# Table addresses of a group computed together at the front of a TensorE step, with the next group's register load behind them

## The chip, the cores and the metric

One NeuronCore of one Trainium2 chip runs the whole kernel. Its engines (TensorE or PE, VectorE or DVE, ScalarE or ACT, GpSimd or POOL, SyncE or SP) have an instruction stream each and meet only at semaphores. On TensorE two things must be kept apart: the sequencer, which executes register instructions, waits and branches, and the array, which takes weight loads (PEld) and matmuls (PE) from a queue that the sequencer fills. The metric is device time in microseconds (us) of one execution.

## The reference

A graph of 3125 nodes with 64 features and 100000 edges, sorted by destination. First three message-passing steps, then three relational layers, with a residual and a layer norm after each part:

```python
h = node_state                                   # three steps
for _ in range(MSG_STEPS):
    msg_in = jnp.concatenate([h[src], h[dst], edge_attr], axis=1)
    msg = _mlp(msg_in, W1e, b1e, W2e, b2e)       # silu(x @ W1 + b1) @ W2 + b2
    agg = jax.ops.segment_sum(msg, dst, num_segments=n) / deg
    h = h + _mlp(jnp.concatenate([h, agg], axis=1), W1n, b1n, W2n, b2n)

def _rgcn_layer(x, W, root, b, src, dst, edge_type, n_nodes):   # three layers
    seg = edge_type * n_nodes + dst
    agg = jax.ops.segment_sum(x[src], seg, num_segments=R * n_nodes)
    agg = (agg / jnp.maximum(cnt, 1.0)[:, None]).reshape(R, n_nodes, -1)
    return x @ root + b + jnp.einsum('rni,rio->no', agg, W)
```

`h[src]` and `h[dst]` are gathers, `segment_sum` is a scatter; these are what the loops below do for every edge.

## The kernel before

The edges are sorted on the chip into tiles of 128 (one block of destinations, one span of 256 sources each), and 8 tiles make a group; there are 160 groups, padding included. Node features stand in SBUF as `table`, split into three bf16 parts (192 columns a block). A gather is a matmul with a one-hot matrix as weights: L934 takes the first 128 sources of the tile's span, L935 the next 128 (`table_next` is `table_flat` shifted by one block row), and L938, in the message layers only, the destination block. The column at which a tile reads the table depends on the data, so it stands in a register of TensorE's sequencer.

The six layers share one pattern: `stage(g, u, i)` is one step and does group g. Layers 0 to 2 are the message layers, 3 to 5 the relation layers. The first four groups of a layer are written out, the other 156 run in a loop of 39 turns with four steps each (u = 0 to 3), and two or three steps without gathers end it.

- In a message layer a step has 24 gather matmuls (8 tiles, L934, L935, L938), 8 transposes of the destination one-hots (L948) and 8 matmuls that sum the messages of group g-3 (L968). Then `load_places` (L916) computes the place of the next group's record and loads nine registers with one TENSOR_LOAD: eight table offsets, and the destination's.
- In a relation layer a step has 8 times two gathers (L934, L935) and four sums of group g-2 (L977). `load_places` (L918, eight registers) stands behind tile 3.

At the front of a step, L988 and L990 clamp the loaded registers (`pe.snap`). A tile's table address is then worked out where the matmul is written: a few additions and multiplications of registers that the builder packs into one instruction (FUSED_REGOPS in the profile, ISA in the program's order) ahead of the matmul. L922 to L926 and L931 compute semaphore values for `gather_ready` (the one-hots of this group have been made or loaded) and for the reading of the previous group's gathers. L1016 is the loop's end.

The other engines work on neighbouring groups meanwhile: VectorE adds the gathered parts (L1337, L1341) and, in the first layer, builds the one-hots (L1315, L1316); ScalarE applies the SiLU and casts; GpSimd forms the low parts and accumulates.

Of the kernel before, what the change touches and what calls it, by code (L numbers as in the profile page):

```python
# [22 lines left out]
K3 = 3 * HID  # L23
# [3 lines left out]
def gnn_kernel(nc, x, src, dst, edge_attr, edge_type, W1e, b1e, W2e, b2e, W1n, b1n, W2n, b2n,  # L27
# [22 lines left out]
    LAYERS = 3  # L50
# [19 lines left out]
    with ExitStack() as ctx:  # L70
# [46 lines left out]
        table_flat = table[:].rearrange("p b m k f -> p (b m k f)")  # L117
        table_next = table_flat[:, ROWW:]
# [258 lines left out]
        def done(n):  # L377

            return n + 1 + PRE
# [407 lines left out]
        def _(pe):  # L787
# [100 lines left out]
            for l in range(2 * LAYERS):  # L888
# [24 lines left out]
                def load_places(g, u, l=l):  # L913

                    if l < LAYERS:
                        pe.load(tile_regs[u % 2] + [dst_reg[u % 2]], places[0:1, bass.ds(ROW * g, GT + 1)])  # L916
                    else:
                        pe.load(tile_regs[u % 2], places[0:1, bass.ds(ROW * g, GT)])  # L918

                def gather_ready(g, u, i, l=l):  # L920
                    if l == 0:
                        pe.wait_ge(ohT_made, done(g))  # L922
                    elif isinstance(g, int):
                        pe.wait_ge(hots_loaded[u], 16 * (QUADS * (l - 1) + g // 4 + 1))
                    else:
                        pe.wait_ge(hots_loaded[u], 16 * (QUADS * (l - 1) + 1) + 16 * i)  # L926

                def gather_tile(g, u, j, off, dst_off, l=l):
                    n = l * NG + g
                    if j % 4 == 0:  # L930
                        pe.wait_ge(gat_read, done(2 * (n - 1) + j // 4))  # L931
                    at = gat[:, 256 * j:256 * j + K3]
                    tile = slice(j * P, (j + 1) * P)
                    pe.matmul(at, ohT[u][:, 0, tile], table_flat[:, bass.ds(off[j], K3)], start=True, stop=False)  # L934
                    ins = pe.matmul(at, ohT[u][:, 1, tile], table_next[:, bass.ds(off[j], K3)],  # L935
                                    start=False, stop=l >= LAYERS)
                    if l < LAYERS:
                        ins = pe.matmul(at, ohT[u][:, 2, tile], table_flat[:, bass.ds(dst_off, K3)],  # L938
                                        start=False, stop=True)
                    if j % 4 == 3:  # L940
                        ins.then_inc(gathered, 1)

                def turn_dst_hots(g, u, l=l):

                    n = l * NG + g
                    pe.wait_ge(hot_out, done(n - 2))
                    for j in range(GT):
                        ins = pe.transpose(oh_ps[u % 2][:, j * P:(j + 1) * P], ohT[u][:, 2, j * P:(j + 1) * P],  # L948
                                           ident_b[:])
                    ins.then_inc(turned, 1)  # L950

                def sums_ready(g, u, l=l):
                    n = l * NG + g
                    pe.wait_ge(acc_read, done(n - 2))
                    if l < LAYERS:
                        pe.wait_ge(hot_out, done(n))
                        pe.wait_ge(low_made, done(n))
                        if l == 0:
                            pe.wait_ge(types_made, done(n))
                    else:  # L960
                        pe.wait_ge(oh_made, done(n - LAYERS * NG))
                        pe.wait_ge(gat_read, done(2 * n + 1))

                def sum_messages(g, u, l=l):
                    w = W3 if l == 0 else K3
                    sums_ready(g, u)
                    for j in range(GT):
                        ins = pe.matmul(accp[u % 2][:, 0:w], oh[u][:, j, :], parts[u][:, j, 0:w],  # L968
                                        start=j == 0, stop=j == GT - 1)
                    ins.then_inc(summed, 1)  # L970

                def sums_half(g, u, j):

                    s = u % 2
                    r = j // 2
                    for t in range(4 * (j % 2), 4 * (j % 2) + 4):
                        ins = pe.matmul(accp[s][:, 256 * r:256 * r + K3], oh4[u][:, t, r * P:(r + 1) * P],  # L977
                                        gb[u][:, t, :], start=t == 0, stop=t == GT - 1)
                    if j == GT - 1:
                        ins.then_inc(summed, 1)  # L980

                def stage(g, u, i, l=l):

                    known = isinstance(g, int)
                    gathers = not known or g < NG
                    off, dst_off = [], None
                    if gathers:
                        off = [pe.snap(r, min_val=0, max_val=SPAN * ROWW * (NS - 1)) for r in tile_regs[u % 2]]  # L988
                        if l < LAYERS:
                            dst_off = pe.snap(dst_reg[u % 2], min_val=0, max_val=ROWW * (NB - 1) + K3)  # L990
                        gather_ready(g, u, i)
                    if l < LAYERS:
                        if gathers:
                            for j in range(GT):
                                gather_tile(g, u, j, off, dst_off)
                            turn_dst_hots(g, u)
                        if not known or g >= LAG:
                            sum_messages(g - LAG, (u + 4 - LAG) % 4)
                        if gathers:
                            load_places(g + 1, u + 1)  # L1000
                    else:
                        adds = not known or g >= 2
                        for j in range(GT):
                            if gathers:
                                gather_tile(g, u, j, off, dst_off)
                            if adds:
                                if j == 0:
                                    sums_ready(g - 2, (u + 2) % 4)
                                sums_half(g - 2, (u + 2) % 4, j)
                            if j == 3 and gathers:  # L1010
                                load_places(g + 1, u + 1)

                load_places(0, 0)
                for g in range(4):
                    stage(g, g, 0)
                with pe.Fori(1, QUADS) as i:  # L1016
                    for u in range(4):
                        stage(4 * i + u, u, i)
                for g in range(NG, NG + (LAG if l < LAYERS else 2)):
                    stage(g, g % 4, QUADS)  # L1020
# [427 lines left out]
```

## Time and profile before

| | |
|---|---|
| median of 3 runs | 5863.55 us (5863.24 to 5865.77) |
| the profiled execution: its time | 5864.59 us |
| its span, first to last instruction | 5862.9 us |
| PE busy | 4725.5 us (81%), 47638 matmuls |
| PEld busy | 4058.5 us (69%) |
| DVE busy | 3972.5 us (68%) |
| ACT busy | 2755.2 us (47%) |
| POOL busy | 3395.9 us (58%) |
| mean granted TensorE clock | 0.863 of 2.4 GHz |
| chain that ended last | PE 56%, POOL 15%, issue 10%, DMA 9%, DVE 7% |

Busy time leaves out register, branch, semaphore and DMA-issuing instructions, so a sequencer full of them looks idle. Such time stands in the chain and in the waits as "issue": the engine waited for nothing that another engine did. Matmul durations overlap, since matmuls are pipelined; their pace is read from the distance of their starts. The sequencer's instructions can be had line by line; there TensorE's have the name PEldq and GpSimd's POOLq.

Until about 1500 us the kernel sorts the edges; then the six layers follow, 640 to 800 us each with what lies between them.

### The profile page before, as it was taken

The numbers are of one execution on the slowest core, as the hardware profiler recorded it, in microseconds if no ns is written. First come the engines' busy times: TensorE is split into PE (matmuls) and PEld (weight loads), VectorE is DVE, ScalarE is ACT, GpSimd is POOL, SyncE is SP. The second block draws the span as 40 slices with busy tenths as digits, with TensorE's granted clock in tenths as the row PEclk, the third lists the DMA queues.
The fourth block names the chain that finished last, engine by engine and source line by source line (L and its number), as shares of the span: only waits on it lengthen the run. The fifth ranks groups of instructions, "written<-read, shape, count | busy, mean of one in ns | idle before, by whom it ended". The sixth has DMA issues, their size and how long they took to land.

```text
span 5862.9 us, 173813 instructions
## 1 busy us (share of the span) xinstructions
PE 4725.5 (81%) x47638; PEld 4058.5 (69%) x47639; DVE 3972.5 (68%) x9658; ACT 2755.2 (47%) x4407; POOL 3395.9 (58%) x4499
## 2 busy tenths in 40 slices
PE   2666666660577777888888888899999999999998
PEld 2444444440466665777767777699998999999997
DVE  6444444440589997777767777688875888578885
ACT  1111111112456665677757777555554555455553
POOL 0777777770367775455535555366653666446663
PEclk9755555555799999999999999899998999899997
DMA  8111111117899997777757777244432444234441
GB/s 327 29 29 29 29 29 29 29 28 244 272 312 333 334 334 245 248 264 266 264 176 265 263 265 265 92 133 133 132 120 83 132 132 133 93 109 133 132 133 58
DMA packets 358467, 975.41 MB, mean 166 GB/s; under 512 B 71168, under 2 KB 83796, under 8 KB 358411
## 3 DMA queue, kind: packets, MB, share of 16 engines
q1 hardware_dynamic: 317352, 946.00, 48.9%
q0 software_dynamic: 38400, 28.13, 2.7%
q10 hardware_dynamic: 2658, 0.51, 0.0%
q8 instruction: 37, 0.61, 0.0%
q14 instruction: 20, 0.16, 0.0%
HBM read 774.54 MB, written 199.06 MB: 166 GB/s over the span
## 4 chain that ended last, share of the span: by engine, by line
PE 56%; POOL 15%; issue 10%; DMA 9%; DVE 7%; another core or an unknown queue 2%; ACT 1%; DVEq 0%; POOLq 0%; SPq 0%; ACTq 0%
PE sums L977 21%; POOL recs L517 14%; PE gat L934 10%; PE gat L935 10%; DMA arena<-rows_d 5%; PE gat L938 4%; PE sums L968 4%; DMA arena<-recs 3%; PE sums L948 2%; DMA recs<-arena 2%; DVE arena L1341 1%; PE gat L1060 1%; DVE arena L1316 1%; DVE arena L1337 1%
## 5 line engine op out<-in xcount | busy, mean ns | idle before, releaser
L934 PE MATMUL gat<-table,arena 128*128 x7680 | 1913.4, 249 | 370.8 <-DVE arena L1341 186.7
L935 PE MATMUL gat<-table,arena 128*128 x7680 | 1916.7, 250 | 0.0
L977 PE MATMUL sums<-arena 128*128 128x192 bf16 x15360 | 1887.2, 246 | 0.0
L1357 DVE TENSOR_SCALAR arena<-iota_s,meta_t 128x512 bf16<-128x512 int16 x3840 | 1523.0, 469 | 363.2 <-PE sums L977 363.2
L977 PEld LDWEIGHTS sums<-arena 128*128 128x128 bf16 x15360 | 1325.3, 98 | 0.1
L517 POOL DMA_INDIRECT recs<-arena x800 | 949.8, 1187 | 377.4 <-issue 374.9
L721 ACT CAST arena<-gat 128x768 bf16<-128x768 f32 x960 | 767.0, 799 | 809.3 <-PE gat L935 809.3
L934 PEld LDWEIGHTS gat<-table,arena 128*128 128x128 bf16 x7680 | 747.7, 97 | 548.3 <-issue 482.1
L938 PE MATMUL gat<-table,arena 128*128 x3840 | 959.9, 250 | 0.0
L540 POOL TENSOR_TENSOR arena<-arena 128x512 bf16<-128x512 f32 x480 | 532.6, 1110 | 726.3 <-ACT arena L707 726.0
L1341 DVE TENSOR_TENSOR arena<-arena,gat 128x256 f32<-128x256 f32 x1920 | 812.0, 423 | 65.8
L935 PEld LDWEIGHTS gat<-table,arena 128*128 128x128 bf16 x7680 | 748.0, 97 | 137.2 <-issue 0.4
L592 POOL TENSOR_TENSOR arena<-arena 128x256 f32<-128x256 f32 x480 | 414.5, 864 | 656.7 <-ACT arena L729 655.9
L693 ACT COPY arena<-sums 128x1024 bf16<-128x1024 bf16 x480 | 486.3, 1013 | 518.2 <-PE sums L948 517.8
L1337 DVE TENSOR_TENSOR arena<-gat,arena 128x256 f32<-128x256 f32 x960 | 402.8, 420 | 263.4 <-PE gat L938 262.1
L832 PE MATMUL gat<-arena 25*125 25x39 bf16 x800 | 232.0, 290 | 401.8 <-DVE arena L1179 401.8
L656 ACT COPY arena<-gat 25x1000 bf16<-25x1000 bf16 x100 | 98.4, 984 | 829.8 <-PE gat L806 807.8
L832 PEld LDWEIGHTS gat<-arena 25*125 25x125 bf16 x800 | 141.2, 176 | 445.9 <-DVE arena L1179 429.7
L598 POOL TENSOR_TENSOR arena<-arena 128x256 f32 x480 | 384.6, 801 | 91.2 <-POOL arena L595 91.2
L968 PE MATMUL sums<-arena 128*128 128x192 bf16 (+1 forms) x3840 | 406.1, 248 | 11.1 <-ACT arena L714 10.9
L729 ACT COPY arena<-sums 128x768 f32<-128x768 f32 x480 | 386.2, 804 | 9.9 <-PE sums L977 9.9
L938 PEld LDWEIGHTS gat<-table,arena 128*128 128x128 bf16 x3840 | 380.3, 99 | 13.4
(184 smaller groups left out, 6228.6 us busy)
## 6 DMA issues: line engine op xcount, KB each, us to landing
arena<-hots_d SPq DMA_DIRECT2D x320, 768.0 KB, 4.5
arena<-hots_d SPq DMA_DIRECT2D x480, 512.0 KB, 3.5
arena<-recs SPq DMA_DIRECT2D x640, 272.0 KB, 3.9
hots_d<-arena SPq DMA_DIRECT2D x160, 768.0 KB, 8.1
arena<-rows_d SPq DMA_DIRECT2D x160, 512.0 KB, 6.9
recs<-arena SPq DMA_DIRECT2D x1, 43520.0 KB, 119.4
recs<-arena POOLq DMA_INDIRECT x800, 2.9
arena<-in_edge_attr_dram SPq DMA_DIRECT2D x100, 62.5 KB
```

The lines of the kernel that those rows point to most:

```text
L517: pool.indirect_dma_start(recs, bass.IndirectOffsetOnAxis(ap=addr_out[s][:, j:j + 1].bitcast(U32), axis=0), rec_out[s][:, j, :], None).the ...
L540: pool.tensor_tensor(parts[u][:, :, 2 * HID:K3], left[s], parts[u][:, :, HID:2 * HID], ALU.subtract).then_inc(low_made, 1)
L693: act.copy(oh[u], oh_ps[u % 2].rearrange("p (j n) -> p j n", n=P)).then_inc(hot_out, 1)
L721: act.copy(gb[u % 4][:, 4 * h:4 * h + 4, :], gat[:, 1024 * h:1024 * h + 1024].rearrange("p (j w) -> p j w", j=4) [:, :, 0:K3]).then_inc(ga ...
L934: pe.matmul(at, ohT[u][:, 0, tile], table_flat[:, bass.ds(off[j], K3)], start=True, stop=False)
L935: ins = pe.matmul(at, ohT[u][:, 1, tile], table_next[:, bass.ds(off[j], K3)], start=False, stop=l >= LAYERS)
L938: ins = pe.matmul(at, ohT[u][:, 2, tile], table_flat[:, bass.ds(dst_off, K3)], start=False, stop=True)
L968: ins = pe.matmul(accp[u % 2][:, 0:w], oh[u][:, j, :], parts[u][:, j, 0:w], start=j == 0, stop=j == GT - 1)
L977: ins = pe.matmul(accp[s][:, 256 * r:256 * r + K3], oh4[u][:, t, r * P:(r + 1) * P], gb[u][:, t, :], start=t == 0, stop=t == GT - 1)
L1337: dve.tensor_tensor(z[s][:, tiles, :], found_parts[:, tiles, 0:HID], rec[:, tiles, 0:HID], ALU.add).then_inc(z_step, 1)
L1341: ins = dve.tensor_tensor(z[s][:, tiles, :], z[s][:, tiles, :], found_parts[:, tiles, m * HID:(m + 1) * HID], ALU.add)
L1357: ins = dve.tensor_scalar(oh4[u][:, j, :], iota_s[:], meta_t[:, bass.ds(GT * g + j, 1), PT - HID], None, ALU.is_equal)
```

## The change

Directly behind the clamps of a step, and before the step's first wait, all addresses of the group are now computed into registers (`pe.lower_ap` on the destination's and on each tile's two table slices); the matmuls later use the same expressions. In the message layers `load_places` for the next group moves from the end of the step to right behind these addresses, so ahead of the gathers. In the relation layers `load_places` stays behind tile 3.

```diff
@@ -988,6 +988,12 @@
                         off = [pe.snap(r, min_val=0, max_val=SPAN * ROWW * (NS - 1)) for r in tile_regs[u % 2]]
                         if l < LAYERS:
                             dst_off = pe.snap(dst_reg[u % 2], min_val=0, max_val=ROWW * (NB - 1) + K3)
+                            pe.lower_ap(table_flat[:, bass.ds(dst_off, K3)])
+                        for r in off:
+                            pe.lower_ap(table_flat[:, bass.ds(r, K3)])
+                            pe.lower_ap(table_next[:, bass.ds(r, K3)])
+                        if l < LAYERS:
+                            load_places(g + 1, u + 1)
                         gather_ready(g, u, i)
                     if l < LAYERS:
                         if gathers:
@@ -996,8 +1002,6 @@
                             turn_dst_hots(g, u)
                         if not known or g >= LAG:
                             sum_messages(g - LAG, (u + 4 - LAG) % 4)
-                        if gathers:
-                            load_places(g + 1, u + 1)
                     else:
                         adds = not known or g >= 2
                         for j in range(GT):
```

What stands on TensorE in a row, in the loop of a message layer, from the sums that end one step to the first tile of the next, before the change (`gat` is where the gathers are written, `places` the table that the registers are loaded from, ISA a packed register instruction):

```order
L968 MATMUL sums<-arena 128x192 x8
L916 ISA
L916 TENSOR_LOAD places
L988 ISA
L931 ISA
L934 ISA
L934 MATMUL gat<-table,arena 128x192
L935 ISA
L935 MATMUL gat<-table,arena 128x192
L938 ISA
L938 MATMUL gat<-table,arena 128x192
```

And with the change:

```order
L968 MATMUL sums<-arena 128x192 x8
L988 ISA
L991 ISA
L994 ISA
L993 ISA x2
L994 ISA x3
L916 ISA
L916 TENSOR_LOAD places
L931 ISA
L934 MATMUL gat<-table,arena 128x192
L935 MATMUL gat<-table,arena 128x192
L938 MATMUL gat<-table,arena 128x192
```

Seven packed instructions (L991 to L994) hold what stood ahead of the 16 matmuls of L934 and L935 and the first of L938; each of the seven has six operations, the ones they replace had two or three. The table load stands behind them, and no register instruction stands between the gathers of four tiles any more.

In the loop of a relation layer, from the last tile of a step to the first tiles of the next, before:

```order
L977 MATMUL sums<-arena 128x192 x4
L988 ISA
L931 ISA
L934 ISA
L934 MATMUL gat<-table,arena 128x192
L935 ISA
L935 MATMUL gat<-table,arena 128x192
L954 REGISTER_ALU
L961 REGISTER_ALU
L977 MATMUL sums<-arena 128x192 x4
L934 ISA
```

And with the change:

```order
L977 MATMUL sums<-arena 128x192 x4
L988 ISA
L993 ISA
L994 ISA x3
L993 ISA x2
L994 ISA
L931 ISA
L934 MATMUL gat<-table,arena 128x192
L935 MATMUL gat<-table,arena 128x192
L954 REGISTER_ALU
L961 REGISTER_ALU
L977 MATMUL sums<-arena 128x192 x4
```

Here six packed instructions have six operations and the last has three; the table load (L918) has kept its place behind tile 3. In the first step of each turn of the loop all seven have six, the last together with the wait's two. The other engines' instructions stand as before.

## Rows read from the trace of the kernel before

**Rows 1.** windows of the span: busy us of each engine, granted clock, DMA
```profile
core 0: us, PE busy (x) PEld busy (x) DVE busy (x) ACT busy (x) POOL busy (x), PEclk, DMA share, GB/s
1512.00:1800.00 288.00, 209.96 (x2197) 173.65 (x2198) 237.86 (x556) 161.24 (x271) 186.17 (x308) 0.93 0.95 311
1800.00:2300.00 500.00, 379.70 (x4190) 310.05 (x4187) 475.95 (x1045) 304.18 (x526) 361.78 (x634) 0.99 0.96 332
2352.00:2992.00 640.00, 565.73 (x6347) 458.17 (x6346) 490.08 (x1113) 452.44 (x790) 354.67 (x620) 1.00 0.79 263
3748.00:4376.00 628.00, 626.94 (x7574) 625.49 (x7574) 505.63 (x1273) 363.69 (x475) 373.59 (x468) 1.00 0.42 132
```

**Rows 2.** waits of PE, 2400 to 2900 us: total, times, longest
```profile
PE gat L934 <- issue: 58.3, 124, 0.8
```

**Rows 3.** chain of waits in one step: start us, us, what
```profile
2502.10 0.45 PE sums L948 x8
2502.55 0.67 PE sums L968 x8
2503.22 0.35 issue
2503.57 0.25 PE gat L934
2503.82 0.13 PE gat L935
...
2504.33 0.08 PE gat L938
```

**Rows 4.** weight loads and matmuls there, in order of time
```profile
2501.87 0.50 PEld L948 LDWEIGHTS sums<-ident_b,arena 128*128 128x128 bf16 x8
...
2502.33 0.66 PEld L968 LDWEIGHTS sums<-arena 128*128 128x128 bf16 x8
...
2503.56 0.10 PEld L934 LDWEIGHTS gat<-table,arena 128*128 128x128 bf16 x1 [0.58 <-issue]
...
2505.82 0.61 PE L948 MATMUL sums<-ident_b,arena 128*128 128x128 bf16 x8
```

**Rows 5.** sequencer by line, 2400 to 2900 us: min/median/max, first and last
```profile
L916 PEldq TENSOR_LOAD <-places x124: 836/843/867, 2401.8 to 2896.3; - x124
...
L988 PEldq FUSED_REGOPS  x93: 165/165/165, 2402.7 to 2893.3; - x93
...
L931 PEldq FUSED_REGOPS  x124: 46/46/60, 2402.9 to 2897.9; - x124
...
L934 PEldq FUSED_REGOPS  x996: 37/37/42, 2400.2 to 2900.0; - x200
```

**Rows 6.** the same for L916 in that step
```profile
L916 PEldq FUSED_REGOPS  x1: 65/65/65, 2502.1 to 2502.1; - x1
```

**Rows 7.** the same in a relation layer, 3800 to 4300 us
```profile
L1016 PEldq COMPARE_BRANCH  x32: 207/208/208, 3807.5 to 4298.5; - x32
...
L962 PEldq EVENT_SEMAPHORE  x95: 51/51/51, 3800.2 to 4295.2; - x95
```

**Rows 8.** the same in one relation step, 4003.3 to 4004.3 us
```profile
L918 PEldq TENSOR_LOAD <-places x1: 592/592/592, 4003.5 to 4003.5; - x1
...
L931 PEldq ALU_OP  x1: 32/32/32, 4004.2 to 4004.2; - x1
```

**Rows 9.** counts by line from 3740 to 4003.39 us
```profile
L934 PEldq FUSED_REGOPS  x524: 42/42/42, 3747.1 to 4002.9; - x175
L934 PEld LDWEIGHTS gat<-table,arena x522: 95/98/152, 3747.2 to 4003.3; 128*128 128x128 bf16 x174
...
L977 PEld LDWEIGHTS sums<-arena x2020: 95/98/98, 3753.5 to 4003.2; 128*128 128x128 bf16 x184
```

**Rows 10.** GpSimd's sequencer, L582, 3800 to 4300 us
```profile
L582 POOLq FUSED_REGOPS  x32: 84/84/84, 3804.4 to 4295.5; - x32
```

**Rows 11.** table loads in the first layer, 1800 to 2300 us
```profile
L916 PEldq TENSOR_LOAD <-places x105: 838/1251/2375, 1800.5 to 2295.9; - x105
```

## The prediction

> **What bounds the kernel now.** I read the stages first, then the waits of TensorE, then the chain inside one step, then the sequencer's own instructions. [rows 1] cuts the span into the first layer (1512 to 2300 us), one of the two other message layers (2352 to 2992 us) and one of the three relation layers (3748 to 4376 us). The reader is to see three limits. In the relation layer TensorE is busy 626.94 of 628 us. In the first layer VectorE is busy 475.95 of 500 us, and DMA at 0.96. In the message layers 1 and 2 nothing is full: PE 565.73 of 640 us, DVE 490.08.
>
> What limits layers 1 and 2 is in [rows 2]: the only wait of TensorE there is "issue", 58.3 us in 124 steps, which no engine ends. [rows 3] shows one step. Gathers follow each other every 0.08 us when they run freely, 8 transposes (L948) take 0.45, 8 sums (L968) 0.67; then comes 0.35 of issue, and the first gathers of the next group come at 0.12 to 0.13 instead of 0.08. The step is 4.02 us on average: 123 intervals between the loads of L916 in 494.5 us [rows 5].
>
> The hole is made by TensorE's sequencer, which works through register instructions and hands matmuls to the array's queue. [rows 4, 5, 6] give its path. L916's packed registers start at 2502.1; the next gather's weights are loaded at 2503.56: 1.46 us. In it run L916 65 ns, the table load 847, L988 165, L931 46 and L934 42 ns, together 1165; what is left, 0.295 us over five steps between instructions, is 0.059 each. The last of the 8 sums' weights was loaded at 2502.33 + 0.66 - 0.10 = 2502.89, so the sequencer was 0.79 us ahead of the array, and the distance from the last sum to the first gather came to 2503.56 - 2502.89 = 0.67 (steady: 0.083). So what counts is the length of sequencer work between the last sum and the first gather, less how far the sequencer is ahead.
>
> **Does the table load hold up what doesn't need it?** It decides all, since the change puts it before gathers whose addresses are ready. In the relation layers it already stands so: at L918, in the middle of a step. [rows 8]: it starts at 4003.5, takes 592 ns (so ends at 4004.1), and the next register instruction, L931, which uses no loaded register, starts at 4004.2. Everywhere else two such instructions are 0.06 apart. So it holds up the sequencer for its whole duration.
>
> **How far ahead can it be?** [rows 9] counts up to 4003.39, just before L918's packed registers. 524 address instructions of L934 are 65 steps of 8 and 4 more, so 524 gather pairs are handed over; 522 pairs have loaded weights: 4 matmuls outstanding. Sums handed over: 63 steps (two have none) of 32, and 16: 2032; 2020 loaded: 12. That is 16 matmuls waiting, in a layer where the array is the limit and the queue has every reason to be full. I take 16 as the most. The Trainium skill (TensorE: Matmul & The Clock Gate, the note on engine queue depths in the section "Architectural detail: the array is 16× 32×32, not 1× 128×128") says TensorE's queue holds 64; even if weight loads and matmuls count apart that is 32 pairs, and the trace disagrees with its 16. What a deeper queue would do is rival D.
>
> **The change, part by part.**
> (a) Removed in every loop step: the register instruction ahead of each L934 and L935 gather (16, and one at L938 in the message layers). Worth something only where they slow the array. In layers 1 and 2 the 24 gathers take 2.25 us up to the first transpose (2503.57 in [rows 3] to 2505.82 in [rows 4]); at 0.083 they take 1.98. I take 0.24 us a step of the 0.27, since a first gather after a hole may stay slow. In the relation layers nothing: the array is full.
> (b) Added at the front of the step: the same 41 or 42 operations, packed in seven instructions of up to six. The nearest six-operation row is L582 on GpSimd, 84 ns [rows 10]; on TensorE two operations take 37 to 42 (L934), three 46 (L931), four 65 (L916) and nine 165 (L988) [rows 5, 6]. That brackets six between 60 (on from two and three) and 110 (two thirds of nine). I take 84, since it is the same count: 7 x (0.084 + 0.059) = 1.00 us. Ends 0.83 and 1.18.
> (c) Moved: the table load (with its 65 ns) goes from behind the sums to behind (b). Still between the last sum and the first gather, so it is neither gained nor hidden.
>
> Layers 1 and 2. The path from last sum handed over to first gather is L988 0.224, (b) 1.00, L916 0.124, load 0.906, L931 0.105: 2.36 us (before 1.46). Against that the sequencer is now free during the gathers and should reach the full 16: 8 transposes and 8 sums, 2501.87 to 2502.89 in [rows 4], 1.02 us, and some 0.03 more. Last sum to first gather: 2.36 - 1.05 = 1.31, was 0.67: +0.64. Less (a): +0.40. With 320 steps: **+130 us** (step 4.02 to about 4.43). Bounds: packed at 60 ns and a lead of 1.10, +0.18, 58 us; packed at 110 and the lead left at 0.79, +0.84, 269 us. No other engine hides it: DVE has 3.1 us of work a step.
>
> Relation layers. Normal step: nothing reaches the array for L988 0.224 + six packed 0.858 + one of three operations 0.105 + L931 0.10 = 1.28 us. The array takes one matmul in 628 us / 7574 = 0.083 [rows 1], so the queue covers 16 x 0.083 = 1.33 and up to 0.08 of the running one: just enough. Then only two gathers (0.165) are handed over before three small instructions ahead of the first sums (32, 32 and 51 ns [rows 7, 8], with distances 0.31 us together): 1.28 + 0.31 against 1.36 + 0.165 leaves 0.07 idle. Every fourth step adds the loop's turn: an ALU operation of 32 ns as in [rows 8] and a branch of 208 [rows 7], 0.092 and 0.267 with their distances, and has seven full packs: 1.69, less 1.36, and 0.31 - 0.165: 0.48 idle. Mean (3 x 0.07 + 0.48) / 4 = 0.17; 480 steps: **+80 us**. The mid-step load (0.77 us with its registers) stays covered, since 18 matmuls (1.5 us) without register work refill the queue before it. Bounds: 20 us (packs at 60 ns: no hole but a third of the loop steps') and 162 us (packs at 110 ns).
>
> First layer. Load durations there are 1251 ns in the median and up to 2375 [rows 11] against 843, so TensorE's own path becomes 4.43 + about 0.5 + 0.12 for L922 (an ALU operation like that of [rows 8], 0.09 with its distance) and the wider sums = 5.05 us; the step is 4.76 now (104 intervals in 495.4 us [rows 11]), of which DVE needs 4.53. +0.29 a step, and of the first 290 us, where the transfers are at 0.95, I count half: **+40 us**, 0 (VectorE or transfers hide it) to +70.
>
> Sum: 130 + 80 + 40 = 250 us on the profiled execution's 5864.6 (span 5862.9, 1.7 around it): **6115 us**, 4.3% slower. That execution is 1 us above the median of the runs. The straight-line groups at the ends of each layer have constant group numbers and hardly change. No DMA, semaphore or other engine's instruction moves.
>
> **Rivals.**
> A: the relation layers stay covered. For it: the normal step lacks only 0.07 us, and the array's queue may hold the one running besides. Then 5864.6 + 130 + 40 + 10 = 6045.
> B: packed instructions are dear (110 ns) or the lead is not gained: for it, mins cost 18 ns each in L988; against, 84 on the other engine. Upper bounds together 269 + 162 + 70, half of the way there from my terms: 6240.
> C: faster, by one mechanism: the table load doesn't hold up the gathers now standing behind it. The place is L931 behind L916 in layers 1 and 2; it decides if less than about 0.5 us of the 0.906 remains. Then the path is 1.45, minus 1.05: 0.40 instead of 0.67, with (a) -0.51 a step, -163 us; the first layer 0; relation +80: 5782. Against it is [rows 8], where it waits with no need.
> D: the queue takes more than 16 matmuls when nothing slows the handing over. With 32 the lead would swallow 2.36 us; the array would run 3.1 us of work a step with DVE's 3.1 beside it, about 3.4: -0.6 x 320 = -192, relation 0, first layer 0: 5673. Against it is [rows 9]. (It is what the Trainium skill's depth of 64 would come to.)
> E: no visible change, when gains and losses cancel: needs (b) at 40 ns per pack, below the two-operation row.
>
> **How the numbers follow.** Forecast 6115: 0.66. A 0.14, B 0.12, C 0.04, D 0.02, E 0.02. The range takes in A and the lower part of B: 6000 to 6240. What a measurement of this kernel can tell from no change is about 0.2%. Faster 0.06, same 0.02, slower 0.92.
>
> **What would show it.** Steps of layers 1 and 2 at 4.4 us between loads, still "issue" as TensorE's only wait, growing from 0.47 to about 1.1 us a step; gathers at 0.08 from the first to the last; seven packed instructions of about 84 ns between L988 and L916; message layers of some 700 us instead of 640. Relation layers: PE no longer without holes, some 655 us instead of 628, holes mainly once in four steps. Wrong would be: L931 starting before the load has ended (C), more than 16 matmuls waiting at L988 (D), packs far from 84 ns (B), relation layers as long as before (A). If the granted clock falls in layers 1 and 2 from 1.00 [rows 1] as far as the first layer's 0.99, it costs under 10 us and changes nothing here.

## The result and the profile after

The changed kernel took 6024.93 us in the median of 4 runs (5974.32, 5990.67, 6059.18, 6066.33), the kernel before, beside it, 5864.45 (5863.24 to 5865.77): a ratio of 1.0245, 95% interval 1.0149 to 1.0340. The ratio compares means and, here and below, leaves out executions more than 1.5% above the shortest of their kernel (6066.33 here), which the medians keep. The changed kernel is slower, since the interval lies above 1; whether by more than 2% these four executions leave open, and six more (again, below) say so, with 1.0230 to 1.0303. 6115 was forecast, 6000 to 6240 the range. The profiled execution is the shortest, 5974.32 us with a span of 5972.6; what follows takes that one apart, and why others take up to 92 us more is a matter of its own (below).

From the page of the kernel after: span and instructions, busy time, and the shares of the chain that ended last.

```profile
span 5972.6 us, 164576 instructions
PE 4620.8 (77%) x47638; PEld 4106.9 (69%) x47639; DVE 3938.1 (66%) x9658; ACT 2778.2 (47%) x4407; POOL 3329.7 (56%) x4499
PE 51%; POOL 14%; DMA 13%; issue 11%; DVE 8%; another core or an unknown queue 2%; ACT 0%; DVEq 0%; POOLq 0%; SPq 0%; ACTq 0%
```

The matmuls are the same 47638; 9237 instructions fewer are executed (173813 before), and the span is 109.7 us longer. Windows of the same stages as in [rows 1], moved along with the layers:

```profile
1512.00:1800.00 288.00, 197.75 (x2218) 178.66 (x2219) 242.11 (x562) 164.08 (x274) 186.88 (x313) 0.95 0.94 313
1800.00:2300.00 500.00, 352.46 (x4184) 318.23 (x4182) 444.41 (x1046) 312.13 (x528) 378.52 (x647) 0.99 0.95 337
2346.00:3020.00 674.00, 516.88 (x6331) 481.24 (x6330) 484.01 (x1110) 460.09 (x790) 313.61 (x621) 1.00 0.74 250
3816.00:4460.00 644.00, 638.77 (x7585) 621.62 (x7583) 503.21 (x1263) 363.92 (x475) 374.84 (x470) 1.00 0.41 129
```

The reader is to see that one message layer now takes 674 us for the work that took 640, and one relation layer 644 for that of 628, with the clock at 1.00 in both kernels. The best measure of a step is the distance between table loads: first and last start in a layer, over 160 intervals.

| us per step | first layer | layer 1 | layer 2 | relation layers |
|---|---|---|---|---|
| before | 4.934 | 4.021 | 4.021 | 3.935, 3.934, 3.935 |
| after | 4.854 | 4.240 | 4.240 | 4.041, 4.020, 4.017 |
| times 160 steps | -13 | +35 | +35 | +44 in the three |

With about 8 us more between the layers that is the 109.7 us of the span.

**Layers 1 and 2.** The waits of TensorE, 2400 to 2900 us (total, times, longest), against [rows 2]:

```profile
PE gat L934 <- issue: 77.6, 89, 0.9
PE gat L934 <- DVE arena L1345: 40.0, 29, 1.4
```

118 steps wait 117.6 us, 1.00 us each (0.47 before). The second row is not VectorE's doing: its 29 times are the loop's turns, every fourth step, where the branch makes the same hole longer (from the last sum's weights to the first gather's 1.71 us, 1.17 to 1.21 in the other steps, read from 2399 to 2455 us), and TensorE's sequencer goes from one register instruction to the next there as elsewhere. The chain in one step, against [rows 3] (start, us, what):

```profile
2500.69 0.45 PE sums L948 x8
2501.14 0.67 PE sums L968 x8
2501.81 0.85 issue
2502.66 0.25 PE gat L934
2502.91 0.08 PE gat L935
```

And what TensorE's sequencer does (by line, min/median/max in ns, first and last start; the first three over 2400 to 2900 us, the others in this step), against [rows 5, 6]:

```profile
L991 PEldq FUSED_REGOPS  x117: 74/74/74, 2402.4 to 2897.0; - x117
L993 PEldq FUSED_REGOPS  x234: 74/74/74, 2402.7 to 2897.4; - x117
L994 PEldq FUSED_REGOPS  x468: 74/74/74, 2402.5 to 2897.8; - x156
...
L988 PEldq FUSED_REGOPS  x1: 165/165/165, 2500.4 to 2500.4; - x1
...
L916 PEldq FUSED_REGOPS  x1: 60/60/60, 2501.5 to 2501.5; - x1
L916 PEldq TENSOR_LOAD <-places x1: 838/838/838, 2501.7 to 2501.7; - x1
...
L931 PEldq FUSED_REGOPS  x1: 51/51/51, 2502.6 to 2502.6; - x1
```

Seven packs of 74 ns, the load, and L931 only when the load has ended (2501.66 + 0.84 = 2502.50). The weight loads of the same step (timeline):

```profile
2500.37 0.10 PEld L938 LDWEIGHTS gat<-table,arena 128*128 128x128 bf16 x1
2500.45 0.51 PEld L948 LDWEIGHTS sums<-ident_b,arena 128*128 128x128 bf16 x8
2500.92 0.66 PEld L968 LDWEIGHTS sums<-arena 128*128 128x128 bf16 x8
2502.65 0.10 PEld L934 LDWEIGHTS gat<-table,arena 128*128 128x128 bf16 x1 [1.07 <-issue]
```

L988 starts at 2500.39, before the first transpose's weights (2500.45). So 8 transposes and 8 sums are all outstanding: 16 matmuls. The two other places of this step where a register instruction stands behind matmuls give the same count: L946 starts at 2503.18, with 24 gathers handed over and 8 loaded, L957 at 2503.84, with 32 matmuls handed over and 16 loaded; each starts 0.02 us after another weight load has begun.

**Relation layers.** The loads of L918 and the branch at the loop's end (L1020 now), 3850 to 4350 us, against [rows 7]; and the weight loads' waits in that stretch:

```profile
L918 PEldq TENSOR_LOAD <-places x123: 587/592/600, 3851.4 to 4348.5; - x123
...
L1020 PEldq COMPARE_BRANCH  x31: 207/208/208, 3857.3 to 4346.0; - x31
```

```profile
PEld gat L934 <- issue: 10.9, 31, 0.4
PEld sums L977 <- issue: 6.3, 31, 0.2
```

31 turns of the loop, 31 holes at the first gather and 31 at the first sums behind it: only one step in four has holes. The others run at 48 matmuls of 0.0825 us, 3.96 us, as before.

### The profile page after: what moved, and what is told of

Read it like the earlier page. It is cut to its first block, busy times and chain, and to the rows that moved or that the text cites. A ratio compares the mean times of both kernels' runs of the same rounds, so it can differ in the third digit from the quotient of the medians.

```text
span 5972.6 us, 164576 instructions
## 1 busy us (share of the span) xinstructions
PE 4620.8 (77%) x47638; PEld 4106.9 (69%) x47639; DVE 3938.1 (66%) x9658; ACT 2778.2 (47%) x4407; POOL 3329.7 (56%) x4499
## 4 chain that ended last, share of the span: by engine, by line
PE 51%; POOL 14%; DMA 13%; issue 11%; DVE 8%; another core or an unknown queue 2%; ACT 0%; DVEq 0%; POOLq 0%; SPq 0%; ACTq 0%
PE sums L977 21%; POOL recs L517 13%; PE gat L934 10%; PE gat L935 8%; DMA arena<-rows_d 8%; PE gat L938 3%; PE sums L968 3%; DMA arena<-recs 2%; DVE arena L1345 2%; PE sums L948 2%; DMA recs<-arena 2%; DVE arena L1341 1%; PE gat L1064 1%; DVE arena L1354 1%
## 5 line engine op out<-in xcount | busy, mean ns | idle before, releaser
L934 PE MATMUL gat<-table,arena 128*128 x7680 | 1903.2, 248 | 580.8 <-DVE arena L1345 312.3
L935 PE MATMUL gat<-table,arena 128*128 x7680 | 1898.1, 247 | 0.0
L934 PEld LDWEIGHTS gat<-table,arena 128*128 128x128 bf16 x7680 | 754.3, 98 | 731.2 <-DVE arena L1345 376.2
L938 PE MATMUL gat<-table,arena 128*128 x3840 | 951.4, 248 | 0.0
L935 PEld LDWEIGHTS gat<-table,arena 128*128 128x128 bf16 x7680 | 756.5, 98 | 0.8
L968 PE MATMUL sums<-arena 128*128 128x192 bf16 (+1 forms) x3840 | 406.5, 248 | 11.5 <-ACT arena L714 11.2
L938 PEld LDWEIGHTS gat<-table,arena 128*128 128x128 bf16 x3840 | 378.6, 99 | 0.5
```

## The experiments

All times are medians in us; ratios are against the kernel before on the same chip (its medians there are 5859.76 to 5862.56). The steps are those of the profiled execution, as in the table above.

| kernel | time (runs) | ratio, 95% | first layer, 1, 2, relation |
|---|---|---|---|
| again (the change unedited) | 6031.12 (6) | 1.0267, 1.0230 to 1.0303 | 4.854, 4.240, 4.239, 4.03 |
| load_last | 6005.54 (6) | 1.0252, 1.0225 to 1.0278 | 5.316, 4.260, 4.253, 4.03 |
| message_only | 5950.90 (4) | 1.0145, 1.0129 to 1.0161 | 4.867, 4.244, 4.243, 3.93 |
| relation_only | 5903.87 (4) | 1.0072, 1.0060 to 1.0085 | 4.931, 4.020, 4.018, 4.02 |
| load_mid | 5735.87 (5) | 0.9784, 0.9771 to 0.9796 | 4.972, 3.452, 3.449, 4.03 |
| halves | 5695.29 (5) | 0.9716, 0.9703 to 0.9728 | 4.907, 3.478, 3.486, 3.93 |
| first_only | 5869.65 (12) | 1.0022, 1.0002 to 1.0043 | 4.864, 4.019, 4.024, 3.93 |
| not_first | 5981.40 (5) | 1.0204, 1.0191 to 1.0218 | 4.932, 4.242, 4.237, 4.02 |
| relation_load_front | 6258.77 (4) | 1.0683, 1.0665 to 1.0701 | relation 4.756 |
| load_early_only | 5870.67 (10) | 1.0020, 1.0010 to 1.0029 | 4.921, 4.021, 4.019, 3.93 |

first_look1 and first_look2 are one more execution each of the kernel of first_only.

### Which layers pay: again, message_only, relation_only

message_only computes the addresses at the front only in the message layers (the load moves as in the change), relation_only only in the relation layers (loads stay where they were).

```diff
-                        for r in off:                            # message_only, against the kernel after
+                        for r in off if l < LAYERS else []:
...
+                        for r in off if l >= LAYERS else []:     # relation_only, against the kernel before
+                            pe.lower_ap(table_flat[:, bass.ds(r, K3)])
+                            pe.lower_ap(table_next[:, bass.ds(r, K3)])
```

> The changed kernel once more, unchanged, for its spread (its four executions so far lay between 5974 and 6066 us, where the kernel before lies within 3 us) and a second profile. Path theory: 4.24 us a step in message layers 1 and 2, 4.02 in the relation layers, 5970 to 5990 us in total; what varies is then in the first layer alone. Rival: what varies lies in all layers alike (a state of the chip or of the clock), and each layer's step is longer by the same per cent in a long execution.

> The change in the message layers alone; the relation layers compute addresses at each matmul, as before. Path theory: relation layers at 3.94 us a step as before, message layers as with the whole change, so the total is that of the changed kernel less 3 x 13 us = about 5935 us. Rival: the relation layers' front costs nothing and the time is that of the whole change.

> The change in the relation layers alone; the message layers as before. Path theory: the loss is in one step of four, where the loop turns (4.3 to 4.4 us instead of 3.96), so 0.08 us a step on average, 40 us in all: 5905 us. Rival: the relation layers are longer in the whole change only because the message layers before them left something behind; then 5865 us. The spread of the executions should be that of the kernel before (3 us), if the spread comes from the message layers.

relation_only costs 41.5 us over the kernel before (5862.33 there) and moves nothing but the relation steps. message_only moves nothing but the message steps. Taking the shortest executions, since the first layer spreads, the two add up: message_only 5937.5, plus 41.5, is 5979.0, and the shortest of again is 5979.6.

### Does the load's place behind the addresses matter: load_last

Addresses stay at the front; the load goes back behind the sums.

```diff
-                        if l < LAYERS:
-                            load_places(g + 1, u + 1)
...
                             sum_messages(g - LAG, (u + 4 - LAG) % 4)
+                        if gathers:
+                            load_places(g + 1, u + 1)
```

> Addresses together at the front of the step, but the table load of the message layers stays behind the sums, as before. Path theory: the same instructions stand between the last sum and the first gather, in another order, so message layers 1 and 2 keep 4.24 us a step and the total is within 15 us of the changed kernel. Rival (the place of the load makes the loss): layers 1 and 2 return to 4.02 us or below and the total to 5880 us or less.

Layers 1 and 2 have the same step (4.26 against 4.24), so in the change as given the load's move is worth next to nothing (the difference of 0.02 us is 5 us over 320 steps): it stays between the last sum and the first gather either way. The whole loss is that of the packs. Its profiled execution was a long one (6049.43), with the excess in the first layer alone.

### Taking the load out of the hole: load_mid, halves, load_early_only

load_mid has the change's addresses and puts the load of the message layers behind tile 3. halves also splits the addresses: tiles 0 to 3 at the front, tiles 4 to 7 in the middle of the step; its load stands behind the last gather.

```diff
-                        if l < LAYERS:                      # load_mid
-                            load_places(g + 1, u + 1)
...
                             for j in range(GT):
                                 gather_tile(g, u, j, off, dst_off)
+                                if j == 3:
+                                    load_places(g + 1, u + 1)
```

```diff
-                        for r in off:                       # halves
+                        for r in off[:4]:
...
-                        if l < LAYERS:
-                            load_places(g + 1, u + 1)
...
                                 gather_tile(g, u, j, off, dst_off)
+                                if j == 3:                  # j == 1 in the relation layers
+                                    for r in off[4:]:
+                                        pe.lower_ap(table_flat[:, bass.ds(r, K3)])
+                                        pe.lower_ap(table_next[:, bass.ds(r, K3)])
+                            load_places(g + 1, u + 1)
                             turn_dst_hots(g, u)
```

> Addresses at the front as in the change, but the table load of the message layers stands behind tile 3's gathers, so under matmuls already in the queue. Path theory: the way from last sum to first gather loses 0.12 + 0.90 of its 2.27 us, so the distance falls from 1.17 to about 0.16 us and a step of layers 1 and 2 would be 3.2 us on TensorE; VectorE with 3.06 us of work then sets it, 3.3 us: 230 us less than before in these two layers, relation layers 40 more, total 5650 us (5600 to 5720). Rival (the packed addresses at the front are what costs, the load being hidden anyway): 4.0 to 4.2 us a step and above 5850 us. If the first layer's spread comes from the load standing in the way between sums and gathers, this kernel's executions lie within 10 us.

> Addresses of tiles 0 to 3 at the front, those of tiles 4 to 7 behind tile 3 (behind tile 1 in the relation layers), table load of the message layers behind the last gather. Path theory: every piece of register work (0.86 us at the front, 0.53, 1.02) is shorter than what 16 queued matmuls cover (1.02 to 1.33), so TensorE has no holes: relation layers back at 3.96 a step also where the loop turns, message layers 1 and 2 at VectorE's 3.3 us or less: 5615 us (5560 to 5680), some 40 below load_mid. Rival: as load_mid in the message layers, and the relation layers not better than with all addresses at the front (4.02).

Both beat both kernels: load_mid by 2.2%, halves by 2.8% against the kernel before. Both miss their expected ranges, by 16 and 15 us, since the steps of layers 1 and 2, at 3.45 and 3.48 us, are longer than I had them. load_mid, waits of the weight loads, 2400 to 2900 us, and its weight loads around the load (timeline; the table load runs from 2499.7 to 2500.55):

```profile
PEld gat L934 <- issue: 30.2, 72, 0.5
PEld gat L934 <- DVE arena L1345: 27.8, 109, 0.3
```

```profile
2500.22 0.10 PEld L935 LDWEIGHTS gat<-table,arena 128*128 128x128 bf16 x1
2500.30 0.10 PEld L938 LDWEIGHTS gat<-table,arena 128*128 128x128 bf16 x1
2500.70 0.10 PEld L934 LDWEIGHTS gat<-table,arena 128*128 128x128 bf16 x1 [0.30 <-issue]
```

The 12 gathers of four tiles, 0.99 us, don't quite cover L931, the packed registers and the load: a hole of 0.30 us stays in such a step. And TensorE now waits for VectorE to read the gathers. From 2400 to 2800 us the weight loads of load_mid wait 24.3 us for issue and 22.2 for VectorE; in halves both are still there, with VectorE's the larger (all engines' waits in that stretch; ScalarE's and GpSimd's, which stand first, are left out):

```profile
...
DVE arena L1348 <- PE gat L938: 30.7, 57, 0.7
PEld gat L934 <- DVE arena L1352: 26.8, 57, 0.6
...
PEld sums L948 <- issue: 14.0, 57, 0.3
PE gat L934 <- DVE arena L1352: 13.0, 50, 0.3
PEld gat L934 <- issue: 9.6, 29, 0.4
...
PE gat L934 <- issue: 0.2, 1, 0.2
```

TensorE waits for VectorE and VectorE for TensorE. "Issue" is gone from the matmuls (0.2 us) but not from the weight loads (14.0 + 9.6 = 23.6 us against VectorE's 26.8). The relation layers of halves are back at 3.93, and that accounts for its advantage: 5735.87 - 5695.29 = 40.6 us, against the 41.5 that relation_only lost. In the profiled executions the first layer (10 us shorter in halves) and layers 1 and 2 (10 us longer) cancel.

load_early_only is the kernel before with one edit: the load goes ahead of the transposes, and the addresses stay in place.

```diff
+                            load_places(g + 1, u + 1)
                             turn_dst_hots(g, u)
...
-                        if gathers:
-                            load_places(g + 1, u + 1)
```

> The kernel before with one edit: the table load of the message layers stands ahead of the transposes (as in halves); each address stays in front of its matmul. Path theory: nothing long stands between sums and gathers any more, but the sequencer never gets ahead, since 17 address instructions pace the gathers: its own work a step is 8 x 0.244 + 0.12 for the tiles, 1.02 for the load, 0.35 for waits, 0.33 for L988 and L931, 0.09 for the loop, together 3.8 to 3.9 us against 3.1 on the array. So layers 1 and 2 at 3.85 to 3.9 us a step instead of 4.02, 5815 to 5830 us in all: the two edits of halves are worth 170 us together and 40 alone. Rival (the place of the load is all that counts): 3.5 us a step as in halves, 5700 us.

The rival's large gain fell, and my smaller one with it: the steps of layers 1 and 2 are 4.021 and 4.019, as before. Its waits of TensorE, 2400 to 2900 us, and its weight loads in one step:

```profile
PE sums L948 <- issue: 86.1, 124, 0.8
```

```profile
2501.48 0.10 PEld L938 LDWEIGHTS gat<-table,arena 128*128 128x128 bf16 x1
2502.44 0.45 PEld L948 LDWEIGHTS sums<-ident_b,arena 128*128 128x128 bf16 x8 [0.87 <-issue]
2502.85 0.65 PEld L968 LDWEIGHTS sums<-arena 128*128 128x128 bf16 x8
2503.49 0.10 PEld L934 LDWEIGHTS gat<-table,arena 128*128 128x128 bf16 x1
```

The hole behind the sums is gone (2503.49 follows without one), as I had said; it has moved ahead of the transposes, with 0.69 us a step where the kernel before has 0.47. The step stays the same because it is the sequencer's own. From 2400 to 2900 us the kernel before has 3170 records on TensorE's sequencer, and from the end of one to the start of the next never more than 0.13 us pass; load_early_only has the same number and the same longest pause. So in both the sequencer never waits for the array in layers 1 and 2, a step is the sum of its register work, and the place of the load can't change that sum. The expectation had put it at 3.8 to 3.9 us, though the 4.02 of the kernel before already was it. The kernel after has 1815 records there and 187 us in pauses of over 0.15 us, in which, by the counts of 16 above, it waits for the array: its work has fallen to 312 us in 500, 2.65 us a step, but the array has to stand still for a block of it.

At the load's place this looks as follows. With its addresses written between the gathers, the sequencer spends 0.244 us on a tile (starts of successive L934 instructions at 2500.313, 0.567, 0.811, 1.055, 1.299) and the array 3 x 0.0825 = 0.248: nothing is gained over eight tiles. The last gather's weights are loaded 0.05 us after the table load has begun (2501.48 against 2501.42). In load_mid and halves the same load is nearly free only because the addresses are out of the way and 12 gathers are handed over in about 0.1 us before it. So it takes both edits together; each alone is worth nothing or less (load_early_only +9 us, load_last as slow as the change).

### How deep the queue is: relation_load_front

relation_only, with the load behind the addresses in the relation layers too.

```diff
                             pe.lower_ap(table_next[:, bass.ds(r, K3)])
+                        if l >= LAYERS:
+                            load_places(g + 1, u + 1)
...
-                            if j == 3 and gathers:
-                                load_places(g + 1, u + 1)
```

> The relation layers alone are changed: addresses at the front, and the table load, which stands under the sums of tile 3 otherwise, is moved to the front behind them. Queue of 16 matmuls, load holding up the sequencer: the front takes 1.22 + 0.77 = 1.99 us against 16 x 0.083 and some 0.06, 1.39 us, of cover; with the three small instructions ahead of the first sums a normal step gets a hole of 0.75 us, one with the loop's turn 1.1: 4.80 us a step in the relation layers instead of 3.94, 6265 us in all. Rival, a queue of 32 pairs (2.6 us of cover): 3.96 us a step, 5870 to 5905 us. Rival, the load doesn't hold up what follows: 4.02 a step, 5905 us.

6258.77 us, within 7 us of the 6265 expected with 16 outstanding matmuls and a load that holds up the sequencer. Waits of TensorE, 3800 to 4300 us, and the chain around the hole:

```profile
PE gat L934 <- issue: 31.8, 78, 0.4
PE gat L934 <- ACT arena L721: 22.1, 26, 0.9
```

```profile
3999.99 0.33 PE sums L977 x4
4000.32 0.41 issue
4000.74 0.25 PE gat L934
```

104 steps wait in it, 78 in the normal steps and 26 in the loop's turns. A deeper queue would have shown none of it: this is the layer in which the array is the limit, so the queue has the rest of the step to fill up. The Trainium skill (TensorE: Matmul & The Clock Gate, section "Architectural detail: the array is 16× 32×32, not 1× 128×128") gives TensorE's queue 64 entries; here 16 matmuls with their weight loads were the most, in this run and at L988 in the kernel after, and the measurement decides.

### The first layer: first_only, not_first, first_look1, first_look2

```diff
+                        if l == 0:      # first_only; l > 0 in not_first: addresses and load of the change, here alone
...
-                        if gathers:
+                        if gathers and not (l == 0):     # not (l > 0) in not_first
                             load_places(g + 1, u + 1)
```

> The change in the first message layer alone. If the spread of the changed kernel comes from the first layer: lowest executions 5845 to 5860 us (a gain of some 10 us), others up to 5950, spread as wide as the whole change's. Rival (the spread needs the longer steps of the later layers or the whole): all within 10 us.

> The change in layers 1 to 5, the first layer as before. Path theory: + 70 us in layers 1 and 2 (4.24 instead of 4.02 us a step), + 40 in the relation layers: 5975 us, all executions within 10 us if the spread is the first layer's. Rival: the same spread of some 90 us as the whole change.

> The change in the first message layer alone, once more for its trace. If the execution is a long one (over 5890 us), the theory expects the excess in a stretch of the first layer in which steps take over 6 us, TensorE's gathers wait for VectorE's one-hots (L1320) and VectorE for TensorE's gathers, with table loads of 2 us and more, as in the 6049 us execution with the load behind the sums; the other layers unchanged. Rival: every step of the first layer a little longer.

> The same kernel a third time, for the same question: the chance that one of the two looks is a long execution is about one half, from 5 of 12 above 5870 us. What is expected is as for the first look.

not_first spreads 7 us (5979.34 to 5986.65), first_only 152 (5852.80 to 6004.75, eight of its twelve executions at or below 5871.23, four above 5900; without the longest it is still 54): the spread of the changed kernel belongs to the first layer. The two single executions fell on both sides, 5852.17 and 5907.25 us. In the first 112 steps they are alike; then, windows of 2100 to 2200 us (busy us of PE, PEld, DVE, ACT, POOL, clock, DMA) and the loads of 2150 to 2250 us, first_look1:

```profile
2100.00:2200.00 100.00, 72.51 (x870) 65.89 (x868) 90.13 (x221) 64.85 (x108) 78.46 (x131) 1.00 0.98 345
...
L916 PEldq TENSOR_LOAD <-places x21: 841/1046/1467, 2152.4 to 2244.5; - x21
```

and first_look2:

```profile
2100.00:2200.00 100.00, 66.03 (x680) 60.89 (x678) 77.41 (x170) 47.68 (x85) 56.83 (x101) 0.88 0.83 271
...
L916 PEldq TENSOR_LOAD <-places x18: 839/2166/2725, 2151.6 to 2249.4; - x18
```

In the long execution 680 matmuls are done instead of 870 and the loads take twice as long. From the 120th step on a step takes 5.9 us in the mean (4.2 to 8.0) where the short execution has 4.6. From 2100 to 2200 us TensorE's matmuls wait 11.5 us for VectorE's one-hots (four times; L1325 in this kernel) and VectorE 19.7 us for the gathers, as expected, but TensorE's largest wait is issue, 21.1 us. The rival, every step a little longer, falls: the steps before are alike. The lower granted clock (0.88) doesn't explain the loads: in halves they are as long at 0.98 (1800 to 2300 us). What starts the second regime in one execution and not in another stays open. A longer load alone isn't enough: halves has loads of 2293 ns in the median in its first layer and spreads 6 us. There the load stands behind gathers that can cover it; that this is the reason is argued, not shown.

## Why the prediction came out as it did

- **The load holds up the sequencer (C).** Right: L931 starts 0.06 us after the load's end in the kernel after; relation_load_front shows it in another layer.
- **At most 16 matmuls ahead (D).** Right, twice, as above.
- **(b) the packs.** Sized too high: 84 ns was taken from GpSimd's row [rows 10]; they take 74, and start 0.1325 us apart. Seven make 0.93 us, not 1.00: 23 us less over 320 steps.
- **The path, 2.36 us.** Measured 2.27 (0.07 of the difference is the packs'), from L988 (2500.39) to the first gather's weights (2502.65).
- **The lead, 1.05 us.** The last sum's weights are loaded 1.10 us after L988 starts (2500.92 + 0.66 - 0.10 = 2501.48). Distance from the last sum to the first gather 1.17 us, where 1.31 was forecast and 0.67 was before: 45 us less in all, half of it the packs'.
- **(a) the gathers.** From the first gather's matmul to the first transpose's 1.99 us (2502.66 to 2504.65, trace of the kernel after), 2.25 before: 0.26 gained, 0.24 forecast.
- **Layers 1 and 2.** Together +0.50 - 0.26 = +0.24 in this step, and +0.22 in the mean: +70 us, where +130 was forecast. Sign and mechanism held. The path (0.09, with the packs), the lead (0.05) and the gathers (0.02) were all off to the same side, 0.16 of the +0.40, and a difference of terms of 1 to 2 us feels that. What the prediction did not say is that the kernel before is bound here by its sequencer alone, which never pauses (load_early_only above); the change takes a third of that work away and still loses, since what is left stands in one block that the queue doesn't cover.
- **Relation layers.** +44 us where +80 was forecast. The loop turn's hole came much as sized: 0.48 us forecast, 0.44 in the first of the three layers (4.40 us between the loads there against 3.96) and 0.35 in the other two (4.32 and 4.31), which over 39 turns each is 45 us, so all of the loss. The hole of 0.07 in the normal step did not come at all. There the margin was 1.28 + 0.31 against 1.36 + 0.165; with packs of 74 ns the left side is 0.06 less, nearly all that was missing. Rival A, which had the layer covered at +10 us, is as near in time (34 us off, the forecast 36): three steps of four are covered.
- **First layer.** -13 us in the shortest execution; +37 if the 50 us between the median and the shortest execution are all put down to it, where +40 was forecast. That agreement is luck: I had one longer path in mind, and what happens is two regimes. With the change in the first layer alone (first_only) the median is 7 us above the kernel before. With not_first's 119 that makes 126, where the whole change has 160 in the median and again 169; whether long executions are more frequent in the whole change or six of its ten and four of first_only's twelve fell so by chance stays open. [rows 11] had shown the load's long tail in the kernel before, but not that it can tip.
- **Sum.** On the shortest execution 70 + 44 - 13 and 8 between the layers, the 109.7 us of the span, against 250. In the median it is 160. The range held the median only by the long executions of the first layer, which the prediction did not have: it does not hold the two shorter ones, at 5974 and 5991.

## What to carry to other kernels

Two things are to be kept apart: how much register work a step has, and where it stands. The kernel before has too much (4.02 us against some 3.1 of matmuls), the changed one little enough (2.65) but in the wrong place. Register work is free as far as the sequencer is ahead of the array at that place, and it gets ahead only over matmuls that need no register work, up to the queue's depth. So take the addresses out of the matmul run and spread them, and the blocking load, in pieces no longer than the lead (here 1.1 us measured over 8 transposes and 8 sums, 1.3 estimated over 16 gathers at 0.0825) over places where the queue has just been filled: the same instructions gave +2.5% in one block and -2.8% in two with the load apart. Before moving one blocking instruction alone, look whether the sequencer ever pauses, and compute the lead at the new place.

## What the runs showed of the hardware

- A TENSOR_LOAD of nine registers takes 835 to 872 ns and one of eight 587 to 608 in every kernel and layer but the first. In the first layer (1800 to 2300 us), where DMA is at 0.94 to 0.96 and VectorE builds one-hots, the load of nine took 1251 ns in the median in the kernel before [rows 11], 983 in the kernel after, and in halves, where it stands at another place in the step:

```profile
L916 PEldq TENSOR_LOAD <-places x105: 842/2293/2989, 1798.5 to 2291.7; - x105
```

- FUSED_REGOPS on TensorE: 74 ns for six operations, 60 for the four of L916, 51 for L931's; GpSimd took 84 for six [rows 10]. An operation count from another engine was 14% too high.
- Matmuls whose addresses are known are handed over in a burst while the queue has room: in load_mid the 12 gathers of four tiles between L931 (2502.75, 51 ns) and L916 (2502.92).
